# A four-layer graph network on one core: the third layer's neighbour sums as two float32r products

## The reference, cut to what matters

```
def gcn(h, W, b): return segment_sum(w[:, None] * (h @ W)[src], dst) + b      # L1 has two of these
def L2(h, norm, W, b):
    x = norm * (h @ W.T + b)
    return segment_sum(x[src], dst) * norm          # norm = max(in-degree, 1) ** -0.5
```

## Time and profile before

| what | value |
|---|---|
| median of 3 runs | 3631.68 us (3629.55 to 3637.06) |
| the profiled execution: its own time | 3632.91 us |
| its span in the trace | 3631.1 us |
| mean granted TensorE clock | 0.938 of full speed |
| TensorE matmul busy over the span | 3303.6 us, 91% |
| VectorE busy | 2295.8 us, 63% |
| ScalarE busy | 850.1 us, 23% |
| the six parts, start to end | 855.9 to 1763.6 us |

### The profile page before, as it was taken

The page is one execution under the profiler, slowest core; times in us unless marked ns, Lnnn a source line. Parts: engine busy times, 40 slices in busy tenths (PEclk is TensorE's granted clock), DMA queues, the critical chain, the costliest instruction groups (busy, mean ns, idle before and its releaser), DMA issues.

```text
span 3631.1 us, 34205 instructions
## 1 busy us (share of the span) xinstructions
PE 3303.6 (91%) x12605; PEld 1842.2 (51%) x12605; DVE 2295.8 (63%) x3020; ACT 850.1 (23%) x1116; POOL 794.5 (22%) x651
## 2 busy tenths in 40 slices
PE   6679985988999999999739999999999999997998
PEld 4567764754544554545514444444444444474444
DVE  9963321344020120535798888888888898877987
ACT  1113331343000001322112222222222222252222
POOL 7888888820000000000101111111111000010000
PEclk6569997998999999999869999999999999998999
DMA  9999997992434344222456556555655432284422
GB/s 325 364 330 284 307 273 175 281 243 81 145 117 142 120 132 154 78 71 68 129 164 165 113 121 147 118 132 118 138 116 130 106 94 73 77 294 128 122 67 66
DMA packets 278001, 572.57 MB, mean 158 GB/s; under 512 B 92265, under 2 KB 156246, under 8 KB 275787
## 3 DMA queue, kind: packets, MB, share of 16 engines
q1 hardware_dynamic: 140795, 432.89, 37.5%
q0 software_dynamic: 84560, 77.50, 13.1%
q10 hardware_dynamic: 52480, 60.01, 5.6%
HBM read 365.44 MB, written 204.86 MB: 157 GB/s over the span
## 4 chain that ended last, share of the span: by engine, by line
PE 41%; DVE 7%; issue 5%; DMA 2%; ACT 1%; POOL 0%; DVEq 0%; ACTq 0%; POOLq 0%
PE ps L1246 28%; PE ps L1085 3%; PE ps L1210 3%; PE ps L1274 2%; PE ps L1253 2%; DVE R L2173 2%; DMA den_d<-R 1%; DVE wB L2136 1%; DVE PT L1968 1%; DVE wA L1968 1%; PE ps L1038 1%; DVE Fb L1968 1%; PE ps L1276 0%; DVE PT L2136 0%; PE ps L1186 0%
## 5 line engine op out<-in xcount | busy, mean ns | idle before, releaser
L1246 PE MATMUL ps<-R,B 125*128 125x500 f32 x2800 | 1093.9, 542 | 32.9 <-DVE R L2173 26.8
L1246 PEld LDWEIGHTS ps<-R,B 125*128 125x128 f32 x2800 | 503.8, 190 | 595.8 <-issue 552.5
L751 POOL DMA_INDIRECT pairs<-w x392 | 606.6, 1548 | 130.8 <-issue 107.1
L1085 PE MATMUL ps<-R,H 125*128 125x500 f32 (+1 forms) x1400 | 542.6, 542 | 15.1 <-ACT H L1357 7.6
L1484 ACT ACTIVATE R<-R,asc 125x1625 f32<-125x1625 f32 (+1 forms) x200 | 320.2, 1601 | 989.7 <-DVE R L2160 989.7
L2160 DVE SCALAR_TENSOR_TENSOR R<-H,asc 125x1625 f32<-125x1625 f32 (+1 forms) x200 | 368.9, 1845 | 144.7 <-PE ps L1253 113.4
L2173 DVE SCALAR_TENSOR_TENSOR R<-R 125x1625 f32<-125x1625 f32 (+1 forms) x250 | 444.8, 1779 | 0.0
L1085 PEld LDWEIGHTS ps<-R,H 125*128 125x128 f32 x1400 | 253.3, 191 | 283.5 <-issue 280.5
L938 PE MATMUL ps<-R,H 125*128 125x375 f32 (+1 forms) x1000 | 300.4, 447 | 49.3 <-DMA R<-pairs 48.8
L1246 PE MATMUL ps<-R,H 125*128 125x500 f32 (+1 forms) x700 | 274.0, 547 | 19.8 <-DVE R L2173 18.1
L781 POOL DMA_DIRECT2D den_d<-R x138 | 117.4, 851 | 794.6 <-DVE R L2173 770.7
(11 more groups left out here) (319 smaller groups left out, 2948.8 us busy)
## 6 DMA issues: line engine op xcount, KB each, us to landing
pairs<-R SPq DMA_DIRECT2D x25, 3200.0 KB, 18.1
R<-ct_d SPq DMA_DIRECT2D x162, 406.2 KB, 3.5
R<-pairs SPq DMA_DIRECT2D x25, 2500.0 KB, 11.3
R<-ct_d SPq DMA_DIRECT2D x162, 375.0 KB, 3.2
R<-wt_d SPq DMA_DIRECT2D x50, 812.5 KB, 4.4
R<-wt_d SPq DMA_DIRECT2D x50, 750.0 KB, 4.1
den_d<-R POOLq DMA_DIRECT2D x75, 312.5 KB, 5.6
den_d<-R POOLq DMA_DIRECT2D x75, 250.0 KB, 4.8
```

What stands on the lines that cost most here:

```text
L751: pool.indirect_dma_start(pairs, bass.IndirectOffsetOnAxis(ap=key_u[:, c:c + 1], axis=0), val[:, c, :], None, compute_op=ALU.add)\
L1085: last = mm(ps[:, bank, at:at + w], rows[0:Q, j, f * 128:(f + 1) * 128], TL[q % TS][0:Q, o:o + w], start=j == 0 and at == 0, stop=j == NB ...
L1246: last = mm(ps[:, bank, at:at + w], rows[0:Q, j, f * 128:(f + 1) * 128], TT[q % TR][0:Q, o:o + w], start=j == 0 and at == 0, stop=j == NB ...
```

## The change

It leaves parts 0 to 3 as they are in their products, and rebuilds what belongs to L2.

- **Rows in two pieces.** `split_rows` copies each normalised row to a float32r tile `BR` (the high part, which the type rounds) and puts the exact rest into another, `HR`. VectorE does it in pairs of blocks, half 0 in part 3 and half 1 in part 4.
- **Units of float32r.** `count_unit` multiplies the cast tile, now float32r too, with `BR` and with `HR`, into the same bank. The fourth chunk is 126 columns wide. There are as many products of 500 columns as there were matmul records before.
- **A 26th unit.** Counts over 4096 are not exact in float32r. VectorE finds the rows that have one (`scan_tile`, `heavy_flags`), ranks them (`rank_rows`, `rank_ids`, with one small product each), GpSimd's queue gathers up to 16 of them, and `rest_counts` works out what the cast left off. `rest_unit` adds it at the end of parts 4 and 5 with gathered rows of `BR` and `HR`, which SyncE's queue has stored to DRAM (`rows_out`, behind the count tiles n = 2 and 20).
- **The norm sums earlier.** `cn` is built in `scan_tile` while L1 runs, from count tiles loaded a second time by SyncE's queue (50 tiles, three in four units, from q = 7 to 72). `source_sums` reduces it to one number per target node in part 3 with 25 products of one column. The bias is then added by VectorE block by block (`add_bias`), and the products of L1041 are gone. `count_tile` is gone too; `own_counts` takes the identity off the uint16 tile, two units ahead and before the cast.
- **Normalising spread out.** ScalarE normalises three or four blocks behind each of four casts, in place of all at once. L3's first 13 blocks go to `Bn0` in `Fb`, and a second time to `Bn` behind part 5.

Smaller things: a few semaphores are merged, and some buffers lie elsewhere. The core of the diff:

```diff
+        SCAN = 2 * NB
+        SCAN_AT = {7 + n * 4 // 3: n for n in range(SCAN)}
...
+            if k == 2:
+                for n, it in enumerate(("ranks", "ids")):
+                    AUX.append((it, None))
+                    PLAN[3][9 + n].append(len(AUX) - 1)
             if k == 3:
...
+            def count_load(m, j, half):
+                c0, w = HALF[half][0] * Q, COLS[half]
+                sp.dma_start(C16[m % CS][:, 0:w], ct_d[j, :, c0:c0 + w]).then_inc(S(f"c16_in{m % CS}"), 16)
+
+            def rows_out(half):
+
+                j0, nj = HALF[half]
+                sp.wait_ge(S("bn_ready"), NB + j0 + nj)
+                for t, rows in zip(hl_d, (BR, HR)):
+                    sp.dma_start(t.rearrange("(j p) f -> p j f", p=Q)[:, j0:j0 + nj, :], rows[0:Q, j0:j0 + nj, :].bitcast(F32))\
+                        .then_inc(S("high_low"), 16)
+
             for q in range(4 * NB):
                 k, j = divmod(q, NB)
                 c0, w = HALF[k % 2][0] * Q, COLS[k % 2]
                 if q >= TS:
                     sp.wait_ge(S("l12_pe"), q - TS + 1)
                 sp.dma_start(TL[q % TS][:, 0:w], wt_d[j, :, c0:c0 + w]).then_inc(S(f"t_in{q % TS}"), 16)
+                if q in SCAN_AT:
+                    m = SCAN_AT[q]
+                    if m >= CS:
+                        sp.wait_ge(S("cn_made"), m - CS + 1)
+                    count_load(m, m % NB, m // NB)
             for q in range(4 * NB, 6 * NB):
                 k, j = divmod(q, NB)
-                c0, w = HALF[k % 2][0] * Q, COLS[k % 2]
                 n = q - 4 * NB
                 if n >= CS:
-                    sp.wait_ge(S("cast"), n - CS + 1)
-                sp.dma_start(C16[n % CS][:, 0:w], ct_d[j, :, c0:c0 + w]).then_inc(S(f"c16_in{n % CS}"), 16)
+                    sp.wait_ge(S("cast"), cast_of(n - CS) + 1)
+                else:
+                    sp.wait_ge(S("cn_made"), SCAN)
+                count_load(SCAN + n, j, k % 2)
+                if n in ROWS_OUT:
+                    rows_out(ROWS_OUT.index(n))

...
+            g.affine_select(out=UPPER, in_=UPPER, compare_op=ALU.is_gt, fill=0.0, base=0, pattern=[[1, Q]],
+                            channel_multiplier=-1).then_inc(S("pool_consts"), 1)
+            pool.wait_ge(S("rest_made"), 2)
+            pool.wait_ge(S("l12_pe"), 4 * NB)
+            by_place, by_node = [bass.IndirectOffsetOnAxis(ap=sel_u[0:RANKS, i:i + 1], axis=0) for i in range(2)]
+            pool.indirect_dma_start(rest_c[:, 0:N], None, ct_d.rearrange("b p n -> (b p) n"), by_place)\
+                .then_inc(S("picked"), 16)
+            pool.wait_ge(S("high_low"), 64)
+            for i in range(2):
+                pool.indirect_dma_start(picked[:, i * D:(i + 1) * D], None, hl_d[i], by_node).then_inc(S("picked_hl"), 16)
...
-                        if layer == 2:
-                            last = mm(ps[0:Q, 7, m * D:(m + 1) * D], cn[h][0:Q, b * Q:(b + 1) * Q], bcs[0:Q, 3, :],
-                                      start=False, stop=True)
+                                      start=f == 0, stop=f == KT - 1)
                 last.then_inc(S("aux_pe"), 1)
...
+            def source_sums(j):
+
+                if j == 3:
+                    pe.wait_ge(S("cn_made"), SCAN)
+                    pe.wait_ge(S("evA"), EVA[3])
+                for b in range(max(2 * j - 6, 0), min(2 * j - 4, NB)):
+                    half = int(b >= HALF[1][0])
+                    at = (b - HALF[half][0]) * Q
+                    o, acc = [(o, acc) for o, acc in cnp[half] if o <= at][-1]
+                    mm(ps[0:Q, 6, 2 * D - 32 + b:2 * D - 31 + b], acc[0:Q, at - o:at - o + Q], ones[0:Q, 0:1],
+                       start=False, stop=True, skip_group_check=True)
+
+            def count_unit(k, j, u, pair, jj, rows):
+
+                pe.wait_ge(S("cast"), u - 4 * NB + 1)
+                for f in range(KT):
+                    for i, part in enumerate(pair):
+                        for c, (o, w) in enumerate(CHUNKS[k % 2]):
+                            bank, at = bank_of(f, c)
+                            if c == 3:
+                                at, w = f * (Q + 1), Q + 1
+                            if j == 0 and i == 0:
+                                bank_free(k, f, c)
+                            last = mm(ps[:, bank, at:at + w], part[0:rows, jj, f * 128:(f + 1) * 128],
+                                      TLr[u % TS][0:rows, o:o + w], start=j == 0 and i == 0 and at == 0,
+                                      stop=j == NB and i == 1, skip_group_check=c == 3)
+                last.then_inc(S("l12_pe"), 1)
+
+            def rest_unit(k):
+
+                pe.wait_ge(S("rest_made"), 3)
+                kept = [rest_r[:, i * D:(i + 1) * D].unsqueeze(1) for i in range(2)]
+                count_unit(k, NB, DONE[k] - 1, kept, 0, RANKS)
...
-                    pe.wait_ge(S("ln_done"), 2 * NB + j + 1)
-                if layer < 2:
-                    pe.wait_ge(S(f"t_in{q % TS}"), 16 * (q // TS + 1))
-                else:
-                    pe.wait_ge(S("cast"), q - 4 * NB + 1)
-                    j0, nj = HALF[half]
-                    if j0 <= j < j0 + nj:
-                        pe.wait_ge(S("minus"), j + 1)
+                    pe.wait_ge(S("bn_ready"), NB + j + 1)
+                    count_unit(k, j, 4 * NB + cast_of(q - 4 * NB), (BR, HR), j, Q)
+                    return
+                pe.wait_ge(S(f"t_in{q % TS}"), 16 * (q // TS + 1))
+                if k == 3:
+                    source_sums(j)
...
+                if k >= 4 and j == NB - 1:
+                    rest_unit(k)
                 if k == 5 and j in EARLY_S:
...
+                u, m = 4 * NB + cast_of(n), SCAN + n
+                j0, nj = HALF[k % 2]
+                act.wait_ge(S(f"c16_in{m % CS}"), 16 * (m // CS + 1))
+                if j0 <= j < j0 + nj:
+                    act.wait_ge(S("minus"), j + 1)
+                act.wait_ge(S("l12_pe"), u - TS + 1)
+                a(TLr[u % TS][0:Q, 0:w], C16[m % CS][0:Q, 0:w], ACT.Copy).then_inc(S("cast"), 1)
                 if j == 2:
                     evac_f0(k - 1)
                 if n == LNAT:
-                    normalise(2, 1, H)
+                    spread(2, 1)
+                if LNAT <= n < LNAT + 4:
+                    j0 = HALF[1][0] + 3 * (n - LNAT)
+                    normal_rows(H, j0, j0 + 3)
+                if j == NB - 1:
+                    act.wait_ge(S("rest_made"), 3)
+                    act.wait_ge(S("l12_pe"), u + 1 - TS + 1)
+                    c0 = HALF[k % 2][0] * Q
+                    a(TLr[(u + 1) % TS][0:RANKS, 0:w], rest_b[:, c0:c0 + w], ACT.Copy).then_inc(S("cast"), 1)
                 if n == NB + 5:
                     act.wait_ge(S("aux_dve"), NORMS + 1)
...
+                    spread(3, 0)
+                if NB + LNAT < n <= NB + LNAT + len(CBE):
+                    j0, nj = CBE[n - NB - LNAT - 1]
+                    normal_rows(Bn0, j0, j0 + nj)
...
+            normal_rows(Bn, 0, NE)

...
+            def own_counts(q):
+
                 k, j = divmod(q, NB)
-                h, w = k % 2, COLS[k % 2]
-                j0, nj = HALF[h]
-                dve.wait_ge(S("cast"), n + 1)
-                t = TL[q % TS][0:Q, 0:w]
...
-                    dg = t[:, (j - j0) * Q:(j - j0 + 1) * Q]
+                    dve.wait_ge(S(f"c16_in{m % CS}"), 16 * (m // CS + 1))
...
+            def scan_tile(m):
+
+                half, j = divmod(m, NB)
+                w = COLS[half]
+                dve.wait_ge(S(f"c16_in{m % CS}"), 16 * (m // CS + 1))
+                link.mark(v_.tensor_reduce(out=most[0:Q, m:m + 1], in_=C16[m % CS][0:Q, 0:w], axis=AX_X, op=ALU.max))
+                if j:
+                    dve.wait_ge(S("cn_made"), m)
+                for o, acc in cnp[half]:
+                    w = min(acc.shape[1], COLS[half] - o)
+                    t, c = C16[m % CS][0:Q, o:o + w], acc[0:Q, 0:w]
+                    if j:
+                        last = stt(c, t, norm[0:Q, j:j + 1], c, ALU.mult, ALU.add)
+                    else:
+                        last = ts(c, t, norm[0:Q, j:j + 1], None, ALU.mult)
+                link.join()
+                last.then_inc(S("cn_made"), 1)
...
+            def rank_rows():
+
+                link(stt(rank[0:Q, :], ladder[1][0:Q, 16:], ps[0:Q, 7, 0:1], flag[0:Q, :], ALU.add, ALU.mult))
+                for r in range(RANKS):
+                    link(stt(junk[0:Q, :], rank[0:Q, :], r + 1.0, named[0:Q, :], ALU.is_equal, ALU.mult,
+                             accum_out=idp[0:Q, r:r + 1]))
...
+            def rest_counts(g):
+
+                n0, w = NCHH[g]
+                dve.wait_ge(S("picked"), 16)
+                c, t = rest_c[:, n0:n0 + w], rest_t[:, 0:w]
+                link(stt(t, iota[0:RANKS, 0:w], sel[0:RANKS, 5 + g:6 + g], c, ALU.is_equal, ALU.subtract))
+                link(cp(rest_r[:, 0:w], t))
```

(92 more changed lines are left out.)

131 lines of the change are left out of this document (88 added, 43 removed).

## The result

The changed kernel takes 3564.2 us (median, 3564.0 to 3567.4), the one before 3631.1 in the same runs: a ratio of 0.982 [0.9805, 0.983], 66.9 us less. The forecast was 3523, its range 3504 to 3558: the change is faster, as forecast, but 42 us of the 109 did not come.

A forecast was written before the change was run, and what follows sets the result against it. TensorE's records were taken to bound parts 3 to 5, VectorE the stretch behind. Terms of -54.9 (part 4), -60.7 (part 5), -5.6 and -2 (bias), +5.6 and waits sum to -109.0 from 3632.9: 3523 us, range 3504 to 3558.

The forecast's parts named there:

- Waits at the start of part 4: Tile 3 queued behind a 12.6 us store makes TensorE wait 6.1 us in place of 2.36: +3.8 us.
- The upper bound: Start of part 4: the store of the rows at 175 GB/s takes 19 us, which makes the wait +10 us.
- The second pair: Part 4, rows_out(1) behind tile 20, 11.6 us long: tile 21 comes nearly in time, +1 us (0 to +6).
- Rival 3: Stores of the rows run at 58 GB/s, 57 and 53 us instead of 12.6 and 11.6: 3603 us, chance 0.04.
- The record of float32r: Parts 4 and 5: a 500-column record takes 0.211 us, so a unit of part 5 takes 2.53 us.
- Rivals 1 and 2: Parts 4, 5: (1) float32r records take two passes, 3644 us, chance 0.07; (2) loads don't hide, 3587 us, chance 0.04.
- the row: Trace row of float32 records of 256 columns at 0.215 us, read as weight loads overlapping matmuls on the same rows.
- the wait for the scales: Part 4, unit 10 waiting for normalised rows: 1.7 us after the change, 1.82 before, so no change.
- the waits forecast beside the stores': Scales in part 4 0, in part 5 +2; bank copies into part 5 +0.8; VectorE in part 5 +1 us.
- source sums: Added TensorE products of one column in part 3 and two small ones, 54 records at 0.103: +5.6 us.
- bias products behind part 5: The 12 target blocks behind part 5 each lose one product with cn: -2 us, at most 5.2, at least 0.
- covered, with 0.8 to spare: Parts 1 to 3: with a scan, VectorE needs 5.9 us where TensorE needs 6.7, so scans cost nothing.

The follow-up runs named there:

- the narrow chunks: The changed kernel with stores cut at partition 112 and the 500-column chunks of parts 4 and 5 cut to 376: 3518.3 us.
- the kernel with both orders: Changed kernel with stores cut at partition 112, ScalarE's bank copies ahead of unit 2's cast, and a VectorE scan ahead of part 0's root item: 3532.2 us, ratio 0.9718.
- the best kernel: The kernel with both orders, its four cut stores spaced out on SyncE, each behind a tile load of its own: 3523.4 us, ratio 0.9694.

## Why the prediction was wrong, step by step

**The step that failed** is the length of the stores under "Waits at the start of part 4": 3250 packets x 0.062 us / 16 = 12.6 us. The price of a packet was taken from stores on ScalarE's queue, and with it the 16. Those stores run over 128 partitions (1250 KB are 128 rows of 2500 float32); `rows_out` stores `rows[0:Q]`, 125. The trace has five engines at work, 3.3 MB at 121 GB/s, 27 us. The upper bound, 19 us, came from the same rows and fell short for the same reason. Put 27 into the prediction's own chain and tile 3 lands 14 us later: a wait of 6.1 + 14 = 20, and the trace has 2.39 + 18.63 = 21.0. The second pair (11.6 us forecast, +1) is in the same way 14 us longer (3.1 MB at 121 GB/s): 15, where the trace has 14.30. The two terms were +4.8 and came out as 33.0: 28.2 of the 42 us. Rival 3 named the store, but with a rate of 58 GB/s, and argued it away by its neighbours.

The Trainium skill (DMA: Bandwidth & Descriptors, Why a DMA increments its semaphore by 16 and not by 1) has the rule: a DMA is spread over the largest number of engines, at most 16, that divides the slowest dimension of both its patterns. For 125 that is 5, for 112 it is 16. The trace agrees: a share of 0.3 uncut, 0.9 while the cut stores run. The forecast didn't weigh it. By it the estimate would have been 3250 x 0.062 / 5 = 40 us, too long, since a packet took 0.041 here.

**The record of float32r** (0.211 forecast) is 0.225: one pass, no exposed load. In part 5 that is 26 x 0.17 = 4.4 us. In part 4 the unit came out at 3.17 as forecast, by luck: long records dearer, short ones cheaper (0.79 - 0.675 = 0.115, not 0.16). Rivals 1 and 2 are out, and by the narrow chunks a bound by transfers too. On loads the row was right. The Trainium skill's rule (TensorE: Matmul & The Clock Gate, Part 3, The mechanism) that a load overlaps a running matmul only where the row groups differ isn't borne out here: all these loads use the same 125 rows, a load lasts 0.19 us, and records of 376 columns, each with its load, start 0.172 apart.

**The clock** was not in the sum. Behind the gaps of 18.63, 1.81, 14.30 and 2.17 us (not behind those of 2.39 and 0.96) records ran for some microseconds at the lower level, 1.2 GHz: the groups of four at 1488.99 and 1490.46 above start 1.47 us apart, not 0.79. From the spacing of groups that is 2.9 us behind the first long gap, 3.2 at two places behind the wait for scales, 2.15 behind the second, 2.2 at the start of part 5: 10.5 us. An estimated 1.5 us of that is not the clock but TensorE catching up with bank copies: the first records at 1487.02 start 0.65 apart, the pace of VectorE's copies, and at the full clock the group at 1466.01, behind ScalarE's, takes 1.43 us for 0.79. The window 1487 to 1550 has a mean of 0.90, 1550 to 1605 of 0.84, where the earlier trace rows had the full clock. The kernel before has gaps of 1.82 and 2.16 us at the two places where the changed one has 1.81 and 2.17, the wait for the scales and the start of part 5, and lost no clock there in its profiled execution. Why these cost clock now is open.

These three terms, 28.2 + 4.4 + 10.5, make 43.1 for the 42.1 missed in parts 4 and 5. That they fit so well is in part luck, since smaller misses cancel: the waits forecast beside the stores' came out 3.6 us shorter (0.2 for 3.8), the items and the units behind them 1.7 longer, and the first group of part 4 took 0.6 more, waiting for bank copies.

**Right:** source sums +6.0 for +5.6; part 4's start ended by VectorE's copies behind a tile's landing, and the 1.8 us wait for the scales (forecast 1.7); bias products behind part 5, -3.6 for -2; ranks and `split_rows` cost nothing that the trace shows in part 3.

**Wrong, but small:** "covered, with 0.8 to spare" held for every scan but one, the one behind part 0's root item, a place where VectorE waits for TensorE: 2.35 us, as the kernel with both orders shows.

That the best kernel lands at 3523.4, the forecast to the microsecond, is chance: it has two orders that the change lacks (5.7 us), and they pay for records and clock. Without its stores the changed kernel had 918.4; the forecast without its 4.8 for them, 906.3.

## What to carry to other kernels

- For each new DMA, read the partition count of both sides and ask on how many engines it runs, before you take a rate from a neighbour: 125 rows ran on 5 of 16, and a cut at 112, one line, was worth 28 us of the stretch.
- A slow DMA costs by what is queued behind it. Moving it to another queue moved the stall to that queue's own next work; one short store per tile, inside the lead of the tiles, made it free.
- Look at the granted clock behind each gap, and not only at the gap. In the changed kernel most gaps of 1.8 us or more in parts 4 and 5 were followed by about 2 to 3 us of loss, two of them at places where gaps as long had cost nothing before.
